# Attention statistics from accumulated squares, a start of zero products on TensorE, and new start orders in a decoder layer on one core

## What is computed

```python
# stage 1: linear attention with a memory (M, z); sigma(a) = elu(a) + 1; x seen as (b, s, h)
q, k, v = x @ w_q.T, x @ w_k.T, x @ w_v.T                     # 512 -> 128
num/den over the causal pairs of sigma(q), sigma(k), v; plus sigma(q) @ M / (sigma(q) @ z)
x = layernorm(x + output @ w_o.T)                             # mean and variance of each token
# stage 2: long convolution of pairwise products of the context, times x
kv = einsum('bhil,bhjl->bijhl', ctx_, ctx_)
y  = causal_conv(kv, ssm_kernel) + kv * D
x  = layernorm(x + einsum('bijhl,bhil->bjhl', y, x_))
# stage 3: gated feed-forward with fp4 weights, then RMS norm
h = silu(x @ w_gate.T) * (x @ w_up.T)
y = h @ w_down.T
x = layernorm(x + y / sqrt(mean(y * y) + eps))
```

## Time and profile before

| | us |
|---|---|
| median of 3 runs (lowest, highest) | 537.48 (537.46, 539.65) |
| profiled execution | 537.01 |
| its span | 535.3 |
| TensorE busy in it | 506.2 (95%) |
| VectorE, ScalarE, GpSimd busy | 383.5, 404.8, 393.2 |

### The profile page before, as it was taken

One profiled execution on the slowest core, in us unless ns is written; L12 is line 12 of the kernel. 1 busy time (PEld: TensorE's weight loads), 2 busy tenths in 40 slices (PEclk: granted clock), 3 DMA queues, 4 the chain that ended last, 5 costly groups with the idle time before them and its releaser, 6 DMA issues.

```text
span 535.3 us, 11731 instructions
## 1 busy us (share of the span) xinstructions
PE 506.2 (95%) x3668; PEld 379.0 (71%) x3668; DVE 383.5 (72%) x1152; ACT 404.8 (76%) x962; POOL 393.2 (73%) x449
## 2 busy tenths in 40 slices
PE   6888998989999999999999999999999999999992
PEld 6676787777786677677767776777677767765660
DVE  2899679988878767776777776768777777763223
ACT  3557673337999888788888897889788877788981
POOL 2679774874897599769968995899589859871231
PEclk9999999999999999999999999999999999999997
DMA  8724667310454662032104110412040111001001
GB/s 222 186 84 94 154 121 209 97 39 2 94 144 80 141 168 87 21 102 78 60 1 117 59 59 0 118 59 59 13 130 14 39 34 46 2 2 41 0 21 39
DMA packets 66146, 40.63 MB, mean 76 GB/s; under 512 B 37882, under 2 KB 55418, under 8 KB 66106
## 3 DMA queue, kind: packets, MB, share of 16 engines
q1 hardware_dynamic: 66106, 40.13, 29.5%
HBM read 27.46 MB, written 12.66 MB: 75 GB/s over the span
## 4 chain that ended last, share of the span: by engine, by line
PE 45%; POOL 24%; issue 19%; DVE 6%; ACT 4%; POOLq 1%; DMA 1%; DVEq 0%; ACTq 0%
POOL shared L297 7%; POOL h_lo L1080 5%; PE p_qk L878 4%; PE p_cv L137 4%; PE p_cv L139 3%; PE p_cv L138 3%; PE p_n L1273 3%; PE p_n L1271 3%; PE p_n L1272 3%; POOL kv L197 3%; PE p_n L889 3%; PE p_x L1258 2%; PE p_qk L1258 2%; PE p_x L1260 2%; PE p_qk L1260 2%
## 5 line engine op out<-in xcount | busy, mean ns | idle before, releaser
L1080 POOL TENSOR_TENSOR h_lo<-w,h_hi 128x256 f16<-128x256 f32 x88 | 70.3, 805 | 44.6 <-ACT h_hi L1129 43.0
L137 PE MATMUL p_cv<-kv_hi,toe 128*128 128x288 f16 x320 | 91.6, 286 | 1.8 <-DVE shared L257 1.8
L138 PE MATMUL p_cv<-kv_lo,toe 128*128 128x288 f16 x320 | 91.5, 286 | 0.0
L139 PE MATMUL p_cv<-kv_hi,toe 128*128 128x288 f16 x320 | 91.5, 286 | 0.0
L1112 ACT ACTIVATE p_qk<-p_qk,rescale 128x256 f32<-128x256 f32 x192 | 78.4, 451 | 12.3 <-PE p_qk L1260 11.7
L297 POOL TENSOR_TENSOR shared<-shared 128x1024 f32<-128x1024 f32 x32 | 75.4, 2358 | 12.0 <-DVE shared L257 12.0
L1112 ACT ACTIVATE p_x<-p_x,rescale 128x256 f32<-128x256 f32 x192 | 78.4, 453 | 6.1 <-PE p_x L1260 5.9
L1112 ACT ACTIVATE p_s<-p_s,rescale 128x256 f32<-128x256 f32 x144 | 58.9, 454 | 11.2 <-PE p_s L1260 11.2
L1271 PE MATMUL p_n<-wd_hi,h_hi 128*128 128x512 f16 x176 | 66.8, 379 | 0.0
L1272 PE MATMUL p_n<-wd_lo,h_hi 128*128 128x512 f16 x176 | 66.7, 379 | 0.0
L1273 PE MATMUL p_n<-wd_hi,h_lo 128*128 128x512 f16 x176 | 66.7, 379 | 0.0
(11 more groups left out here) (161 smaller groups left out, 1262.7 us busy)
## 6 DMA issues: line engine op xcount, KB each, us to landing
toe<-toeplitz_rows SPq DMA_DIRECT2D x16, 512.0 KB, 3.8
cnat<-in_ctx SPq DMA_DIRECT2D x16, 256.0 KB
xq<-x_blocks SPq DMA_DIRECT2D x16, 256.0 KB, 6.2
xr<-x_rows SPq DMA_DIRECT2D x16, 256.0 KB
out_x<-fin SPq DMA_DIRECT2D x16, 256.0 KB
ring<-in_x SPq DMA_DIRECT2D x6, 512.0 KB, 4.1
x_rows<-ring SPq DMA_DIRECT2D x6, 512.0 KB, 2.9
x_blocks<-ring SPq DMA_DIRECT2D x48, 64.0 KB
```

Of the source, the lines that this page charges most:

```text
L137: nc.tensor.matmul(dst, hi, kh, start=(mb == 0), stop=False)
L138: nc.tensor.matmul(dst, hi, kl, start=False, stop=False)
L139: done = nc.tensor.matmul(dst, lo, kh, start=False, stop=(mb == lb))
L1080: nc.gpsimd.tensor_tensor(h_lo[:, i, :], h32[:, i % 2, :], h_hi[:, i, :], ALU.subtract).then_inc(h_low, 1)
```

## The change

The change touches the start part alone; the lists of the periods stay as they are. It has three parts.

1. **Statistics of the attention's layer norm.** The two `bn_stats`, the two `bn_aggr` and the small operation behind them on DVE go. The residual addition also puts out the sum of each row (`total`); `bm` makes the negated mean from it; `qs` on ACT squares the row minus its mean and puts out the sum (`dev`); `bn` is now one small DVE operation that makes the variance. `nb` multiplies the negated mean by the root, as a `tensor_tensor` instead of a `scalar_tensor_tensor`.
2. **Products of zeros.** DVE first clears 512 fp16 columns, and PE multiplies them eight times before its first transposition.
3. **New orders** for all five engines in the start part, with additional waits where the tile `sq` is now shared between the parts.

```diff
         def root(i):
-            pool.wait_ge(stats, i * 5 + 5)
+            pool.wait_ge(stats, i + 1)
...
+        def deviations(i):
+            act.wait_ge(mean_made, i + 1)
+            for e in range(2):
+                nc.scalar.activation(sq[:, e], ring[i % RING][:, e, :], ACT.Square, bias=negmean[:, i, e:e + 1],
+                                     accum_out=dev[:, i, e:e + 1]).then_inc(deviated, 1)
...
-            nc.vector.tensor_tensor(r, (p_n0, p_n1)[e][:], r, ALU.add).then_inc(z_made, 1)
-
-        def statistics(i):
-            for e in range(2):
-                dve.wait_ge(z_made, 2 * i + e + 1)
-                nc.vector.bn_stats(st[:, i, e, :], ring[i % RING][:, e, :]).then_inc(stats, 1)
-            for e in range(2):
-                dve.wait_ge(stats, i * 5 + e + 1)
-                dve.sem_inc(cv.seen, 1)
-                nc.vector.bn_aggr(mv[:, i, e, :], st[:, i, e, :]).then_inc(stats, 1)
-            dve.wait_ge(stats, i * 5 + 4)
-            nc.vector.tensor_scalar_add(ve[:, i, :], mv[:, i, :, 1], LN_EPS).then_inc(stats, 1)
+            nc.vector.scalar_tensor_tensor(out=r, in0=(p_n0, p_n1)[e][:], scalar=1.0, in1=r, op0=ALU.mult, op1=ALU.add,
+                                           accum_out=total[:, i, e:e + 1]).then_inc(z_made, 1)
+
+        def means(i):
+            dve.wait_ge(z_made, 2 * i + 2)
+            nc.vector.tensor_scalar(negmean[:, i, :], total[:, i, :], -1.0 / D, None, ALU.mult).then_inc(mean_made, 1)
+
+        def variances(i):
+            dve.wait_ge(deviated, 2 * i + 2)
+            nc.vector.tensor_scalar(ve[:, i, :], dev[:, i, :], 1.0 / D, LN_EPS, ALU.mult, ALU.add).then_inc(stats, 1)
...
+            dve.wait_ge(mean_made, i + 1)
+            nc.vector.tensor_tensor(shift[:, i, :], negmean[:, i, :], rs[:, i, :], ALU.mult).then_inc(shifted, 1)
...
+            if name == "ze":
+                nc.vector.memset(zeros, 0.0).then_inc(zeros_made, 1)
...
+        def keep_busy():
+
+            pe.wait_ge(zeros_made, 1)
+            for k in range(8):
+                nc.tensor.matmul(p_n1[:], zeros[:, 0:P], zeros, start=True, stop=True)
...
-    START_ACT = ("kw0 xa0 kw1 xb0 kw2 kw3 re0 vk0 ks0 ge0 xa1 xb1 lc0 rv0 wh0 wh1 ok0 wh2 re1 wh3 kt0 xa2 vk1 xb2 wh4 "
...
+    START_ACT = ("xa0 kw0 kw1 xb0 kw2 kw3 re0 ge0 vk0 ks0 xa1 xb1 lc0 rv0 wh0 wh1 re1 ok0 kt0 wh2 rv1 wh3 qs0 xa2 vk1 "
```

More of the change, by code:

```diff
@@ L358, in first_stage @@
     shift = sb("shift", [P, SLOTS, 2], F32)
+    total, negmean, dev = (sb(n, [P, SLOTS, 2], F32) for n in ("total", "negmean", "dev"))
+    sq = keep["sq"]
     p_qk, p_x, p_s, p_n0, p_n1 = bank
@@ L373, in first_stage @@
     unpacked, gate_exp, factored = sem("unpacked"), sem("gate_exp"), sem("factored")
+    zeros_made = sem("zeros_made")
+    zeros = cv.kv_lo[0][:].rearrange("p r m c -> p (r m c)")[:, 0:512]
     w_scaled, w_flipped, w_high, w_low = sem("w_scaled"), sem("w_flipped"), sem("w_high"), sem("w_low")
@@ L644, in step @@
                 keep_oT(i)
+            elif name == "qs":
+                deviations(i)
             elif name == "nm":
@@ L790, in step @@
             name, i = named(s)
-            if name == "u":
+            if name == "ze":
+                nc.vector.memset(zeros, 0.0).then_inc(zeros_made, 1)
+            elif name == "u":
                 dve.wait_ge(*((in_pg, 16) if i < 3 else (in_pd, 16)))
@@ L814, in step @@
                 residual(i, 0 if name == "ra" else 1)
+            elif name == "bm":
+                means(i)
             elif name == "bn":
-                statistics(i)
+                variances(i)
             elif name == "nb":
@@ L950, in step @@
             name, i = named(s)
-            if name == "iw":
+            if name == "ze":
+                keep_busy()
+            elif name == "iw":
                 flip_projection(i)
@@ L1001, in periods @@
     h_lo = sb("h_lo", [P, GI, NT], F16)
-    sq = sb("sq", [P, GT, D], F32)
+    sq = keep["sq"]
     z3, fin = keep["z3"], keep["fin"]
@@ L1137, in square @@
             act.wait_ge(y_done[t], f + 1)
+            if isinstance(f, int) and f == 0:
+                act.wait_ge(*free[6])
             nc.scalar.activation(sq[:, t], p_y[t][:], ACT.Square, accum_out=ss[:, t]).then_inc(y_squared[t], 1)
@@ L1190, in add_residual @@
                 dve.wait_ge(*free[4])
+                dve.wait_ge(*free[-2])
             nc.vector.scalar_tensor_tensor(out=z3[:, t, :], in0=p_y[t][:], scalar=rr[:, t], in1=x2hold[:, t, :],
@@ L1205, in finish @@
                 dve.wait_ge(*free[5])
+                dve.wait_ge(*free[-1])
             nc.vector.tensor_scalar(fin[:, t, :], z3[:, t, :], mv3[:, t, 0:1], rs3[:, t], ALU.subtract,
@@ L1312, in decoder_layer @@
     x1_blocks = nc.dram_tensor("x1_blocks", [2 * NG, 4, P, P], F32, kind="Internal").ap()
-    START_SYNC = ("x3 x4 cx3 tw0 cx2 toe0 st0 st1 x5 st2 st3 x6 xq0 cx5 toe1 xr1 xr0 x7 cx4 xq1 toe2 xq2 xq3 toe3 xq5 "
-                  "st4 cx6 xr2 xq4 cx7 toe4 xr3 st5 st6 st7 toe5").split()
-    START_PE = ("Xa0 iw0 iw1 iw2 Xb0 iw3 iz0 Q0 V0 S0 Xa1 M0 N0 Xb1 w0 w1 Q1 T0 f0 w2 w3 Oa0 Xa2 Ob0 w4 S1 w5 V1 Xb2 "
[8 rows of a table removed]
-                "+y0_6 +y0_7 +y0_8 +y0_9 +xt1 +y0_10 +d0 +d1").split()
-    START_DVE = ("is0 u0 sg0 mk0 ig0 dn0 fs0 o0 u1 ra0 sg1 rb0 mk1 u2 dn1 sk0 o1 bn0 ra1 rb1 sg2 bn1 mk2 nb0 nb1 dn2 "
[5 rows of a table removed]
-                 "+bs0 +gu7 +kq1 bn7 +bn0 +gu8 +bs1 +nm0 +bn1 +gu9 nb6 +gu10 +nm1 +xt0 +ln nb7 +xt1 +a0 +b0 +e0").split()
@@ L1332, in decoder_layer @@
[L1332 removed]
[7 rows of a table removed]
[L1340 to L1344 removed]
+    START_SYNC = ("x3 x4 cx2 st0 cx3 tw0 x5 st1 st2 x6 st3 toe0 xq0 xq2 toe1 xq1 x7 cx5 cx4 xr1 xr0 toe2 st4 cx6 xq3 "
+                  "xr2 toe3 xq5 xr3 st5 toe4 xq4 cx7 st6 toe5 st7").split()
@@ new lines, in decoder_layer @@
+    START_PE = ("ze0 Xa0 iw0 iw1 iw2 Xb0 iw3 Q0 iz0 V0 S0 Xa1 M0 N0 Xb1 w0 w1 Q1 T0 w2 f0 w3 Oa0 Ob0 Xa2 S1 V1 w4 w5 "
[8 rows of a table added]
+                "+y0_6 +xt0 +d0 +y0_7 +y0_8 +y0_9 +xt1 +y0_10 +d1").split()
+    START_DVE = ("ze0 is0 u0 sg0 mk0 ig0 dn0 fs0 o0 u1 sg1 ra0 rb0 bm0 mk1 u2 dn1 bn0 o1 kl0 nb0 sg2 ra1 rb1 bm1 mk2 "
[6 rows of a table added]
+                 "+xt0 +xt1 +a0 +b0 +e0").split()
+    START_ACT = ("xa0 kw0 kw1 xb0 kw2 kw3 re0 ge0 vk0 ks0 xa1 xb1 lc0 rv0 wh0 wh1 re1 ok0 kt0 wh2 rv1 wh3 qs0 xa2 vk1 "
[8 rows of a table added]
+                 "+hh10 nm7 +xt1 +n0").split()
@@ L1404, in decoder_layer @@
             "z3": sb("z3", [P, GT, D], F32),
+            "sq": sb("sq", [P, GT, D], F32),
             "fin": sb("fin", [P, GT, D], F32),
```

17 lines of the change are left out of this document (7 added, 10 removed), and 42 rows, old and new, of tables (START_ACT, START_DVE, START_PE).

## The result

| | before | after |
|---|---|---|
| median of 20 runs each (lowest, highest), us | 538.36 (536.94, 541.29) | 537.27 (536.44, 537.94) |
| profiled execution, its span | 537.01, 535.3 | 537.01, 535.3 |
| TensorE busy in it | 506.2 | 508.7 |

The ratio is 0.9976 (95% interval 0.9965 to 0.9987): 1.3 us, a quarter of the 5.0 that were predicted. The medians hide something. The times of the kernel before fall into two groups: ten of these 20 runs lie near 537.4, ten near 539.5. Those of the changed kernel form one group, and its median is that of the lower group of before (537.41). So set against the lower group the change is worth nothing, and the question is where 5 us went.

The account below looks back on a forecast made before the run. TensorE's 11.6 us of idle before its steady stretch, and half-clock products, were nearly all to be won; 0.8 + 0.9 + 1.8 + 2.2 - 0.7 = 5.0 us, so 532.5 us, forecast 530 to 534.5, wider range 529.0 to 537.5.

Parts of the forecast that it names:

- Zeros: At the start, eight products of zeros raise TensorE's clock before the weights land; Q0 at 8.25 instead of 9.06: 0.8 us.
- Rival 5: At the start, the zeros do not lift the clock: 0.8 us less gain, 533.3 us, inside the forecast's own range.
- cover of 0.6 us: Per slot, V products of 2.02 us hide mean and squares of 1.4 us; beyond 0.6 us each late tenth costs a tenth.
- 9 to 43 us: First four slots in the new orders: earlier u1, sigma and V1 win 0.9 of TensorE's 2.50 idle us.
- 43 to 85 us: Pair products moved on GpSimd and VectorE free of three statistics: 1.8 us, less than half of TensorE's idle 4.39.
- 85 to 128 us: Gain of 2.2 us: the 1.3 us wait for slot 6's output goes, and 0.9 of the other 2.6 idle us.
- VectorE's relief: From 85 to 128 us, VectorE has 1.45 us less per slot for two or three slots; 0.9 us gained.
- 128 to 176 us: Squares of slot 7 add 1.22 us to a ScalarE with 3.7 us of rest; loss of 0.7 us.
- 1: Rival: all cover holds in the start part, some 9 us gained, 528.5 us; chance 0.10.
- 2: Rival: VectorE's 16 additional small operations, blocked by GpSimd, and accumulator reads give the gain back; 535 to 537 us; chance 0.18.
- 3: Rival: ScalarE, 92% filled in the first period, cannot follow; 2 to 3 us lost, 534.5 to 536 us; chance 0.09.
- 4: Rival: toe0 and xq0 queue behind slot 3's stores, c0 waits beyond 2.5 us of slack; up to 541 us; chance 0.11.

Follow-up runs that it names:

- short_squares: The changed kernel with all sixteen squares over 8 of the 512 columns, variances not the reference's: 536.51 us, 0.9975 of the kernel before.
- output_copy_first: The changed kernel with the transposed output's copy again ahead of the exponent on ScalarE for slots 0 and 1: 536.28 us, 0.9962 of the kernel before.

## Why the prediction was wrong, point by point

- **What bounds the kernel.** Right in that the end moves with TensorE's idle time ahead of its steady stretch. It left out that half of the executions of before are 2 us longer; the shown median, 537.48 us of three runs with 539.65 among them, was that of the lower group. I read the third run as scatter.
- **Zeros: 0.8 us.** The mechanism held, the size in the profile did not: four transpositions take 0.66 us from the start, but `Q0` starts at 8.58 and not at 8.25, 0.48 us earlier than before; TensorE waits 0.18 us for the second weight and 0.18 for the copy of x. In the runs the zeros are worth 1.0 us on the new lists (537.27 against 538.26); on the old ones 0.5 us between the lower groups and 1.2 between the upper. By the clock records of the traces the clock rises at 7.39, 8.72 and 9.62 us in the three profiles without zeros, at 3.99 to 7.25 in the 17 with them (the windows print 1.00 also ahead of that rise, where nothing is recorded). So the profile of before that I had is the earliest of three, and "high by then", at 4.6 us, came true in 3 of 17: that it did in the changed kernel's is luck. Rival 5 is refuted.
- **Statistics.** The single lines of the changed kernel that answer to the earlier trace rows (times, duration ns min/median/max):

```profile
L775 DVE SCALAR_TENSOR_TENSOR ring<-p_n,ring x12: 666/691/692, 25.1 to 143.7; 128x512 f32<-128x512 f32 x12
L775 DVE DVE_READ_ACCUMULATOR ring<-p_n,ring x12: 75/82/83, 25.8 to 144.3; 128x1 f32 x12
L624 ACT ACTIVATE sq<-ring,negmean x12: 705/722/728, 27.0 to 153.3; 128x512 f32<-128x512 f32 x12
L624 ACT ACTIVATION_READ_ACCUMULATOR sq<-ring,negmean x12: 180/187/205, 27.6 to 153.9; 128x1 f32 x12
```

  VectorE's accumulator read is 0.08 us (I took 0.1). A square takes 0.72 us from start to start, not 0.61: its nearest row read from p_n without a bias, these read the ring with one. That is 1.44 us per slot instead of 1.22; short_squares shows that all of it is worth 0.5 us. The cover of 0.6 us failed at slot 2, where mean and squares took 1.28 + 1.44 = 2.7 us instead of 1.4, against 2.0 for `V2`; most of the excess is the blocked mean.
- **9 to 43 us: +0.9.** Measured -1.6 by idle time; `Q2` stands at 30.79 (29.5 expected), the fourth `Q` at 43.63 (41.4 expected, 43.14 before). Three steps failed. The exponent ahead of `ok`: I let it lower one gain to 0.5 us and then took it as paid; output_copy_first shows that undoing it twice is worth 0.7 us. The cover of mean and squares at slot 2: 0.5 us by two runs. And `V1`, which I put at 25.5, stands at 26.59 as before: `u1` starts 0.48 us earlier and ends when it did, because beside GpSimd's copies its three last operations take 0.91, 0.97 and 0.88 us (0.43, 1.00 and 0.88 before).
- **43 to 85 us: +1.8.** 2.3 measured: right in size. 1.8 was a guess ("less than half"), so the closeness is in part luck.
- **85 to 128 us: +2.2.** 0.2 by idle time. The wait of 1.3 us went as I said. The step that failed is the 0.9 us of VectorE's relief, and the term that it left out: what the wait was moved to. I did not follow the chain behind it, `c0`, terms, trees, x2, `xt1`, x_lo: it starts 2.0 us later, and TensorE meets it at 119 and 127 us, 0.7 and 1.4 us long. VectorE's relief bought little there: the waits for its terms went from 1.5 to 0.8 us, and the chain's start and GpSimd's trees ate it. This is read from the traces; no run puts `c0` back without other losses.
- **128 to 176 us: -0.7.** -1.5 by idle time. The sign is right, the reason was wrong: the load of the squares was named, and taking it away changes nothing. The waits stand at banks to which the new order returns too soon; what bounds the stretch in sum is open.
- **Rivals.** 1 is out. 2 gave 535 to 537 and comes nearest to the time, but by luck: its mechanism explains only some 0.5 us of it. 3 named the right stretch and the wrong cause. 4 did not happen: `c0` waited for no DMA.

The sum by measured terms of the profile: +0.5 (start), -1.6, +2.3, +0.2, -1.5, which is nothing, and nothing is what the two profiles differ by. Term by term the forecast was missed by 0.3, 2.5, -0.5, 2.0 and 0.8 us, in all 5.1. By the runs it reads: the zeros give 1.0 us, and orders and statistics together lose 0.9 against the lower group, where 4.2 were forecast. The 1.3 us of the ratio come from a term that the prediction didn't have: ten of 20 executions of before are 2.1 us longer, and those of the changed kernel are not.
